# Half projections ahead of two attentions, one stage for the hyperbolic attention, and three pairs of score banks

## What is computed

```python
x = x + L0_attn(layernorm(x))            # landmark attention
x = x + L0_xattn(layernorm(x), ctx)      # causal self attention and cross attention, 16 heads of 16
x = x + L0_ffn(layernorm(x))             # linear layer in a 6 bit grid
x = x + L1_attn(layernorm(x))            # hyperbolic attention, causal, 16 heads of 16
x = x + L1_xattn(layernorm(x), ctx)      # mha a1 on x itself, then mha a2 on ctx, 16 heads of 32
x = x + L1_ffn(x)                        # top 2 of 8 experts
```

## Time and profile before

| | us |
|---|---|
| median of 3 runs | 3841.73 |
| lowest and highest | 3839.04, 3848.53 |
| the profiled execution | 3852.28 |
| its span, first to last instruction | 3850.5 |
| PE busy | 3279.7 (85% of the span) |
| VectorE busy | 2066.1 (54%) |
| ScalarE busy | 1651.3 (43%) |
| GpSimd busy | 916.9 (24%) |

### The profile page before, as it was taken

One profiled execution on the slowest core, in us unless ns is written; L12 is line 12 of the kernel. 1 busy time (PEld: TensorE's weight loads), 2 busy tenths in 40 slices (PEclk: granted clock), 3 DMA queues, 4 the chain that ended last, 5 costly groups with the idle time before them and its releaser, 6 DMA issues. The chain is left out here.

```text
span 3850.5 us, 57114 instructions
## 1 busy us (share of the span) xinstructions
PE 3279.7 (85%) x21920; PEld 1798.1 (47%) x21920; DVE 2066.1 (54%) x4278; ACT 1651.3 (43%) x2497; POOL 916.9 (24%) x966
## 2 busy tenths in 40 slices
PE   6888788899898788898897788999897788975997
PEld 4325445235325545244335535254335535254997
DVE  5575655644666664635656664635656665732111
ACT  3353933343354833343345742433356642431332
POOL 1202912011203712011204622011105522023111
PEclk9899799999998899999998899999998898985998
DMA  4113021111203022011203022011211022025997
GB/s 123 38 33 83 1 47 66 49 34 45 58 13 82 1 47 93 21 38 49 60 10 76 1 47 93 21 39 47 62 44 39 1 47 93 22 89 194 333 327 243
DMA packets 250142, 270.61 MB, mean 70 GB/s; under 512 B 96198, under 2 KB 215988, under 8 KB 247572
## 3 DMA queue, kind: packets, MB, share of 16 engines
q1 hardware_dynamic: 202288, 207.46, 18.5%
q10 hardware_dynamic: 44180, 50.17, 4.1%
q0 software_dynamic: 3408, 9.34, 0.6%
HBM read 199.87 MB, written 67.05 MB: 69 GB/s over the span
## 5 line engine op out<-in xcount | busy, mean ns | idle before, releaser
L881 ACT ACTIVATE prob<-psum 128x1024 f32<-128x1024 f32 x384 | 372.2, 1021 | 513.3 <-PE psum L799 513.3
L1262 ACT ACTIVATE prob<-psum 128x1024 f32<-128x1024 f32 (+3 forms) x384 | 331.2, 914 | 367.7 <-PE psum L1151 367.7
L927 DVE TENSOR_REDUCE scr<-psum 128x1 f32<-128x512 f32 x576 | 369.4, 685 | 198.9 <-PE psum L786 195.0
L1304 DVE TENSOR_REDUCE stats<-psum 128x1 f32<-128x512 f32 (+3 forms) x576 | 332.2, 619 | 143.6 <-PE psum L1139 140.5
L796 PE MATMUL psum<-stack 32*128 32x512 f32 x1536 | 226.6, 660 | 15.3 <-ACT prob L881 10.4
L1139 PE MATMUL psum<-stack 96*128 96x512 bf16 (+3 forms) x576 | 183.8, 367 | 31.5 <-DVE stats L1304 31.2
L412 PE MATMUL psum<-ident 128*128 128x128 f32 x1664 | 204.9, 278 | 2.7 <-ACT stack L2222 2.7
L412 PEld LDWEIGHTS psum<-ident 128*128 128x128 f32 x1664 | 197.1, 193 | 15.0 <-issue 7.5
L829 PE MATMUL psum<-prob,ones_f 128*32 128x512 f32 x1536 | 203.4, 598 | 0.0
L1166 PE MATMUL psum<-prob,vbig 128*32 128x512 f32 (+3 forms) x1536 | 191.1, 570 | 0.0
L1693 POOL TENSOR_TENSOR xo<-xa,rows 128x256 f32<-128x256 f32 x32 | 22.2, 725 | 660.3 <-POOLq L69 660.3
(11 more groups left out here) (489 smaller groups left out, 6381.9 us busy)
## 6 DMA issues: line engine op xcount, KB each, us to landing
ew<-in_L_ffn_W SPq DMA_DIRECT2D x39, 1024.0 KB, 6.7
ew<-in_L_ffn_W ACTq DMA_DIRECT2D x39, 1024.0 KB, 7.9
stack<-q_terms SPq DMA_DIRECT2D x144, 128.0 KB, 2.6
w_mlp<-in_L_xattn_a_li_w SPq DMA_DIRECT2D x16, 1024.0 KB, 6.5
q_terms<-parts SPq DMA_DIRECT2D x96, 128.0 KB, 2.2
stack<-k_terms SPq DMA_DIRECT2D x72, 128.0 KB, 3.0
stack<-k_terms SPq DMA_DIRECT2D x36, 256.0 KB, 4.3
w_mlp<-a_terms SPq DMA_DIRECT2D x36, 256.0 KB, 5.0
```

The lines of the kernel that those rows point to most:

```text
L881: act.activation(prob[:, i % 4, :, :], psum[:, 2 * p:2 * p + 2, :], ACT.Exp, scale=scale).then_inc(exped, 1)
L927: dve.tensor_reduce(found[:, c:c + 1], ring(i), AX.X, ALU.max).then_inc(freed, 1)
L1262: act.activation(prob[:, i % 4, :, q0:T], psum[:, 2 * p:2 * p + 2, q0:T], ACT.Exp, scale=scale).then_inc(exped, 1)
L1304: dve.tensor_reduce(found[:, c:c + 1], ring(i)[:, 0:keys_of(t)], AX.X, ALU.max).then_inc(freed, 1)
```

## The change

Four edits, quoted at their core.

**Three pairs of banks.** In the last group of Ba, Bca, e1 and e2 the scores' two pairs of banks rotate through banks 0-1, 2-3 and 4-5, and a score waits for one exponential less.

```diff
+    def score_bank(n, j, kts):
+        m = n - (HG - 1) * kts
+        return j if m < 0 else 2 * ((2 * m + j // 2) % 3) + j % 2
+
+    def exps_before_score(n, kts):
+        return 2 * n if n <= (HG - 1) * kts else 2 * n - 1
...
-                        pe.wait_ge(exped, 2 * n)
+                        pe.wait_ge(exped, exps_before_score(n, kts))
...
-                    if next_products and g == HG - 1 and 3 <= kt < 7:
-                        pe.wait_ge(divided, HG - 2)
-                        for t, k in next_products[2 * kt - 6:2 * kt - 4]:
+                    if next_products and g == HG - 1 and 4 <= kt < 7:
+                        pe.wait_ge(divided, HG - 1)
+                        for t, k in next_products[2 * kt - 8:2 * kt - 6]:
                             join_attention(pe, t, k)
```

```diff
+    def project_half(pe, bank, w, src, g, h):
+        part, kn = slice(h * BANK // 2, (h + 1) * BANK // 2), w.shape[1]
+        for c in range(kn):
+            last = pe.matmul(psum[:, bank, part], w[:, c, g * P:(g + 1) * P], src[:, c, part],
+                             start=(h == 0 and c == 0), stop=(c == kn - 1), skip_group_check=True)
+        return last
...
-        in_a_quad, since, asked = 3 if terms is None else 2, 0, 0
+        in_a_quad, since, asked = 3 if terms is None else 4, 0, 0
...
+                    if i < BEGUN:
+                        project_half(pe, i, w, src, g, 1).then_inc(projected, 1)
+                        return
... Do
+            e.keep_running(pe, 26, 6)
+            turn(0)
+            e.keep_running(pe, 8, 6)
+            pe.wait_ge(e.slot_loaded[1], 96)
+            pe.wait_ge(first_half_in, KT)
+            e.project_half(pe, 0, e.w1q, xT, 0, 0)
+            e.project_half(pe, 2, e.w1q, xT, 1, 0)
+            pe.wait_ge(first_half_in, 2 * KT)
+            e.project_half(pe, 1, e.w1k, yT2, 0, 0)
+            turn(1)
+            e.project_half(pe, 3, e.w1k, yT2, 1, 0)
+            e.keep_running(pe, 3, 6)
... u1
-                e.keep_running(pe, 28, 0)
+                e.keep_running(pe, 8, 7)
+                pe.wait_ge(e.slot_loaded[2], 32)
+                pe.wait_ge(xT_in, 3 * KT)
+                for g in range(HG):
+                    e.project_half(pe, g, e.w2q, xT, g, 0)
+                e.keep_running(pe, 8, 7)
```

```diff
+            turn_first(0)
+            turn_first(1)
             score(0)
-            turn_strips(1)
-            turn_strips(2)
+            turn_first(2)
+            turn_first(3)
             for i in range(-2, NU + 8):
                 if i + 2 < NU and i + 2 in last_unit and units[i + 2][0] + 1 < len(quads):
                     score(units[i + 2][0] + 1)
-                if i == 0:
-                    turn_strips(3)
+                if 0 <= i + 2 < len(strip_halves):
+                    turn_half(i + 2)
... DVE
                 if i + 2 < NU:
                     above_one(i + 2)
+                if 0 <= i + 1 < QT:
+                    value(i + 1)
... ACT
+            take_half(0)
             for i in range(NU + 3):
                 if i < NU:
                     log_of_square(i)
...
-                if i < 2:
-                    take_strips(i + 2)
+                if i < 3:
+                    for n in ((1, 2), (3, 4), (5,))[i]:
+                        take_half(n)
```

More of the change, by code:

```diff
@@ L1220, in _ @@
                 spread_inverses(pe, HG - 1, inverted, spread_in)
-                keep_running(pe, 6, 3)
+                for t, k in next_products[10:]:
+                    join_attention(pe, t, k)
+                keep_running(pe, 2 if next_products else 6, 3)
             @block.scalar
@@ L1460, in twice_normed @@
     HALVES = ((0, 1), (2, 3))
-    with stage(nc, "Do", "joined", "added", "dc", "var_ready", "rstd_ready", "normed", "turned") as (
-            block, joined, added, dc, var_ready, rstd_ready, normed, turned):
+    (xT, _g, _b), (yT2, _g, _b) = turns
+    with stage(nc, "Do", "joined", "added", "dc", "var_ready", "rstd_ready", "normed", "turned", "first_half_in") as (
+            block, joined, added, dc, var_ready, rstd_ready, normed, turned, first_half_in):
         @block.tensor
@@ L1466, in _, with turn @@
                 join_heads(pe, t, HG - 1).then_inc(joined, 1)
-            for h in range(2):
-                e.keep_running(pe, (26, 18)[h], 6)
+            def turn(h):
                 pe.wait_ge(normed, 2 * h + 2)
@@ L2136, in standard_attention @@
                    stack[:, 4096:12288].rearrange("p (s j n) -> p s j n", s=2, j=J), add=e.colB[:, 0, :], ready=2,
-                   next_products=[(t, k) for k in range(HG - 1) for t in range(QT)], beside=add_bias)
+                   next_products=[(t, k) for t in range(QT) for k in range(HG - 1)], beside=add_bias)
 def fp6_linear(e):
@@ L2299, in hyperbolic_attention @@
     QS, KS = (e.work[:, i * 2048:(i + 1) * 2048].rearrange("p (g n) -> p g n", g=HG) for i in range(2))
+    both = e.work[:, 0:4096].rearrange("p (i g n) -> p i g n", i=2, g=HG)
     wide = [e.work[:, i * 2048:(i + 1) * 2048].rearrange("p (t h w) -> p t h w", t=QT, h=H) for i in (2, 3)]
@@ L2484, in by_head @@
         return v[:, 0:units[i][4] * keys(i)].rearrange("p (j n) -> p j n", n=keys(i))
-    with stage(nc, "Da", "scored", "over", "wready", "logged", "rooted", "summed", "far", "squared_dve", "squared_act", "exped", "keep_in", "keep_ready", "turned",
-               "copied", "weighed", "dc", "lifted", "gathered", "inverted", "spread_in", "divided", "strips", "strips_in") as (
-            block, scored, over, wready, logged, rooted, summed, far, squared_dve, squared_act, exped, keep_in, keep_ready, turned,
-            copied, weighed, dc, lifted, gathered, inverted, spread_in, divided, strips, strips_in):
+    strip_halves = [(g, i) for g in range(1, HG) for i in range(2)]
@@ L2500, in score, with turn_first @@
+            def turn_first(t):
+                if t == 1:
+                    pe.wait_ge(imp_in, 1)
+                if t >= 2:
+                    pe.wait_ge(first_in, t - 1)
+                for i, built in enumerate((q_wide, k_wide)):
+                    pe.wait_ge(built, t + 1)
+                    last = turn_strip(pe, i, 0, i * P, 7 - t % 2, t)
+                last.then_inc(first_strips, 1)
             def score(q):
@@ new lines, in _ @@
+            then_mapped(square_sums(QT - 1))
+            then_mapped(dve.tensor_scalar(nmin, nmin, 1e-8, None, ALU.max))
+            dve.sem_inc(least, 1)
+            then_mapped(dve.tensor_scalar(below_one, nmin, 1.0, None, ALU.min))
+            series = ((small_c, (3628800.0, 40320.0, 720.0, 24.0, 2.0)), (small_s, (39916800.0, 362880.0, 5040.0, 120.0, 6.0)))
+            for dst, terms in series:
+                last = dve.tensor_scalar(dst, below_one, 1.0 / terms[0], None, ALU.mult)
+            then_mapped(last)
@@ new lines, in _ @@
+            for i in range(1, 5):
+                for dst, terms in series:
+                    last = dve.scalar_tensor_tensor(dst, dst, 1.0 / terms[i], below_one, ALU.add, ALU.mult)
+                then_mapped(last)
+            for dst, terms in series:
+                last = dve.tensor_scalar(dst, dst, 1.0, None, ALU.add)
+            dve.tensor_scalar(pick, nmin, 1.0, None, ALU.is_lt)
+            dve.wait_ge(rooted, 1)
+            then_mapped(dve.reciprocal(per_root, nroot))
+            dve.wait_ge(both_exped, 2)
```

300 lines of the change are left out of this document (143 added, 157 removed).

## The result

The changed kernel takes 3785.29 us in the median of 4 runs (3779.52 to 3791.31), the kernel before 3842.53 (3839.04 to 3848.53): ratio 0.985, interval 0.983 to 0.987, 57 us less. The forecast was 3799, 42.6 less than before. The profiled execution took 3779.52 us.

What follows compares the result with a forecast made beforehand. PE was taken to bound the kernel (85% busy), except in Da, where ACT does. Terms summed to 10.65 us per pass, four times 42.6, off the 3841.73 median: forecast 3799, range 3778 to 3825.

Steps and rivals of the forecast that it cites:

- u1's small loss: In u1, second transposes come 0.2 us late and ACT's copies behind them end the stage: 0.2 us lost per pass.
- Banks in Ba, Bca, e1, e2: Last groups' scores wait for one exponential less: 0.95, 2.9, 1.3 and 1.3 us gained per pass.
- a price for it: From e2's passes: half of each half-clock microsecond is lost where PE sets the pace; used in a slower rival, chance 0.06.
- Halves in e1: At e1's front, half projections cost PE 3.6 us less, moving quads, maxima and first score forward: 3.6 us gained per pass.
- Halves in e2: In e2's front, the third quad waits for ACT's copy held by the stores: 0.8 us lost per pass.
- the one for a third quad at half clock: In e2, PE's idle gap returns it to half clock and the third quad runs so: 0.8 us lost.
- the one without it: In e2, the third quad does not meet half clock: 0.15 us lost.
- The line drawn for being wrong: In e2, half clock lasting over 25 us would show the forecast wrong.
- halves pay in e2 too: Rival in e2: stores land early, 3.7 us more gained per pass, 3784 us in all; chance 0.20.
- Do and u1: Fewer `keep_running` rounds pay for the half projections: even in Do, 0.2 us lost in u1.
- Joined stage: De and Da in one stage: earlier logs leave a lead of 1.6 us per pass once ACT is full.
- the distance's lead: In Da, the distance at 1243.52 comes 1.6 us earlier, where POOL last held ACT.

Runs made afterwards that it cites:

- banks: Kernel before with only the rotated score banks, including Bca's pieces and Cq's new banks; 36.5 us faster (30 to 43 by its interval).
- the halves alone: Kernel before with only the half projections and `in_a_quad` at 4; 6.5 us faster.
- filled: Changed kernel with `keep_running` in two idle gaps of e2's front, 16 rounds before the third quad and 8 before group 0's turn; 3780.98 us, ratio 0.9829.
- stage: Kernel before with only De and Da joined in one stage; single runs 3820.45 to 3850.53 us.
- before_warm: Kernel before with 8 rounds of `keep_running` on bank 6 ahead of e2's turn of group 0; 3832.54 us, ratio 0.9977.

## Why the prediction was right, and where it wasn't

The forecast, 3799, was 14 us too high; the range (3778 to 3825) held the time. The waits that it named went away where it said, and each of its terms came out in sign except u1's small loss. By its own steps, per pass:

- **Banks in Ba, Bca, e1, e2: forecast 0.95, 2.9, 1.3, 1.3.** At equal half clock 0.7 to 1.0, 3.0, 1.4 and 1.7, some 28 us over the four passes where 25.8 were forecast. The mechanism and the size were right. The part alone gave 36.5 (30 to 43 by its interval). What the forecast missed here is that half clock was booked nowhere as a gain. I had a price for it (half of each cold microsecond where PE sets the pace; 0.38 measured) and used it only for a loss. In the trace of `banks`, e2 lost 5.8 us of half clock behind its first score, 2.2 us of time, Cq in three passes of four its 3.4 us, 1.2 in the mean, and Ba gave 2.0 in all, where 0.7 to 1.0 are the wait. Against these stand a pass of Bca with 30.7 us of half clock, 160.3 us long instead of 151.0, and 0.9 us more ahead of Asm. The timed executions show only 10 us less half clock than before, 3 to 4 us. With the 28 that leaves about 5 us of the 36.5 unexplained, within the interval.
- **Halves in e1: forecast 3.6.** The first score comes 3.4 earlier. The stage gained 3.4 with the part alone (101.8 to 98.4) and 3.0 on top of the banks (100.35 to 97.3).
- **Halves in e2: forecast a loss of 0.8.** The new wait is there with each of its links, and the part up to the first score went from 28.1 to 29.0, a loss of 0.8 to 1.0 (29.1 with the halves alone). Of the two sums that I set side by side, the one for a third quad at half clock (0.8 lost) came out; the one without it (0.15 lost) was on the low side, as the third maximum in `filled` stands at 11.8 to 11.9 where it stood at 11.95 before, so nothing is lost. And the gap also kept what the banks alone had won: half clock behind the first score is 5.7 us with the banks and 10.7 in the changed kernel, 1.9 us a pass. The line drawn for being wrong, 25 us of half clock in e2, was crossed in two passes (27.3); the mean, 23.9, stayed below it. The rival "halves pay in e2 too" falls: the stores landed as late as ever.
- **Do and u1: forecast even, and a loss of 0.2.** Do is 16.9 us in all kernels. In u1 there is no loss: 49.73 with the halves alone, 49.74 before. The 0.4 us that the table shows for the changed kernel stand in `stage` too (49.36), which has u1's instructions unchanged. What does this stays open.
- **Untouched stages.** The stretch from u2 to the next pass's Asm grew from 59.1 to 60.7 us, with 6.8 us of half clock instead of 1.1: the same kind of term with the other sign.
- **Joined stage: forecast 1.6.** Alone 2.2 as a mean (145.6 to 152.5 in single passes), in the whole 3.5 over `banks`. Here too the half clock must be held equal. At 47.8 us of it the stage took 150.8 apart (2 passes of all kernels here) and 148.5 joined (9), at 51.2 it was 150.9 (8) and 149.0 (1), at 58.0 153.6 (4) and 150.9 (4): a gain of 1.9 to 2.7. The two passes of 146.6 have 37.5. The term was somewhat too small; the distance's lead is 3.4 and not 1.6, and where the rest of it goes behind the distance wasn't traced.
- **The whole.** 28 (banks), 4 times 3.0 (e1), 4 times -0.8 (e2) and 4 times 2.2 (stage) are some 46 us. The four timed runs of the changed kernel (0.940 to 0.941) have about 20 us less half clock than those of the kernel before, 6 us at 0.28. That comes to 52 where 57 and 53 were measured. So of the 14 us by which the forecast missed, some 3 or 4 are terms that were too small, about 6 are the clock, which nothing in the forecast foresaw and which could as well have come out the other way, and the rest is within the noise.

The prediction weighed the Trainium skill, "TensorE: Matmul & The Clock Gate", section "HAM oscillation — how this bites in real kernels": idle gaps between bursts bring half clock back. The runs bear it out behind the turn: with that gap filled, half clock there went from 11.5 us to none (`before_warm`). In the changed kernel half clock begins before that gap: at 1501.6, inside the row of quads. The last long gap, the 4.04 us ahead of the third quad, had ended at 1490.94, 10.7 us earlier; from 1495.04 on PE had worked 1.14 us of each 2.2, with 1.06 idle. Busy time of that stretch, to be held against the earlier trace rows:

```profile
1501.60:1522.10 20.50, 15.15 (x60) 3.59 (x61) 10.70 (x17) 3.88 (x4) 0.00 (x0) 0.50 0.00 1
```

## What to carry to other kernels

Write a stage's forecast twice, once at the clock it has and once without its half clock, and count the difference as a chance on both sides: an edit that shifts work by a few microseconds can win or lose such a stretch in stages that it doesn't touch. Judge an edit by its own stage in passes with equal half clock, not by the whole time, and look at several passes, for it also counts where the half clock falls: Bca with the new banks and 3.4 us of it takes 150.9 to 151.0 us in nine passes and 152.5 in three. When work is moved out of a stage's front, follow the oldest DMA there: 1.5 MB of loads, issued ahead of a store that everybody waits for, took back all of 3.6 us, and half of them moved behind it gave it back.

## What the runs showed of the hardware

A microsecond of half clock cost 0.38 us in e2 behind the first score, 0.45 in Cq (1.54 for 3.41), and next to nothing where VectorE sets PE's pace; over whole executions it went with 0.28. Eight rounds of `keep_running`, which compute nothing, take 4.8 us out of the old e2 (174.0 to 169.2). Two stores of 128 KB each landed 5.1 us after their issue behind 1.5 MB of loads, and 2.3 us behind half as much. Stages without half clock repeat to 0.1 us over passes and runs (e1 with the banks alone: 100.31 to 100.40).
